# Macaron block on one core: a linear recurrence in groups of two time steps, its tables in PSUM, x loaded by rows and its statistics carried along

## The reference

```python
logits = tokens @ gate_w                       # [4096, 8]
expert_idx = argmax(softmax(logits))
pos = cumsum(one_hot(expert_idx), axis=0) - 1  # place in the expert, kept below 160
h = relu(einsum('ecd,edf->ecf', expert_input, w1))   # 128 -> 512
expert_output = einsum('ecf,efd->ecd', h, w2)        # 512 -> 128
```

```python
Bu = einsum('bsd,nd->bsn', u, B_w)
h_new = ifft(lambdas * fft(h)).real + bu_t      # 512 steps
y = einsum('sbn,dn->bsd', hs, C_w) + D * u
```

## Time and profile before

| | us |
|---|---|
| three runs | 151.61, 151.71, 152.92 (median 151.71) |
| profiled execution: its own time, its span | 150.5, 148.6 |
| busy: PE, PEld, DVE, ACT, POOL | 128.5, 96.6, 88.2, 56.1, 56.0 |
| chain that ended last: PE, DMA, issue, ACT, POOL, DVE | 46%, 14%, 10%, 9%, 7%, 5% of the span |

### The profile page before, as it was taken

How to read it: one execution, slowest core, us unless ns; L and a number is a source line. 1 busy time by engine, 2 the same in 40 slices (tenths; PEclk the granted TensorE clock), 3 DMA queues, 4 the chain that set the end, 5 groups by cost and what they waited for, 6 DMA issues and landing times.

```text
span 148.6 us, 2493 instructions
## 1 busy us (share of the span) xinstructions
PE 128.5 (86%) x749; PEld 96.6 (65%) x749; DVE 88.2 (59%) x379; ACT 56.1 (38%) x156; POOL 56.0 (38%) x96
## 2 busy tenths in 40 slices
PE   5988989699799989379999999999989969999920
PEld 2315334289699965137887788778976249999810
DVE  1198787994467431257679668988894133755310
ACT  2522434235353302055756675752010035553200
POOL 3490002777205778001212211231100677665570
PEclk9999999999999999999999999999995599999995
DMA  4999995236660111690013441344024312211110
GB/s 89 305 351 401 350 290 144 55 108 185 194 203 22 57 53 53 213 321 35 2 45 101 146 133 39 123 148 146 0 76 158 91 46 56 56 38 40 43 45 18
DMA packets 15740, 18.49 MB, mean 124 GB/s; under 512 B 1904, under 2 KB 10608, under 8 KB 15600
## 3 DMA queue, kind: packets, MB, share of 16 engines
q1 hardware_dynamic: 13936, 15.34, 32.7%
q0 software_dynamic: 1280, 2.66, 6.3%
q10 hardware_dynamic: 512, 0.34, 0.9%
HBM read 12.70 MB, written 7.73 MB: 138 GB/s over the span
## 4 chain that ended last, share of the span: by engine, by line
PE 46%; DMA 14%; issue 10%; ACT 9%; POOL 7%; DVE 5%; SPq 4%; POOLq 1%
PE pair L1062 9%; PE pair L1075 9%; ACT u L520 7%; DMA w1s<-w 5%; PE pair L1158 5%; POOL xg L370 5%; PE pair L1149 4%; SPq L292 3%; PE pair L1180 3%; PE pair L1182 3%; PE pair L943 2%; DMA xg<-x,tok 2%; DMA x<-x_scratch 2%; DMA xg<-x_scratch,tok 2%; PE pair L1087 2%
## 5 line engine op out<-in xcount | busy, mean ns | idle before, releaser
L943 PE MATMUL pair<-warm_in,ones_bf 128*128 128x512 bf16 x61 | 18.9, 457 | 3.9 <-DMA x<-x_scratch 2.3
L1062 PE MATMUL pair<-xcT,w1s 128*128 128x160 f32 x128 | 20.5, 303 | 0.6 <-ACT xcT L452 0.6
L1062 PEld LDWEIGHTS pair<-xcT,w1s 128*128 128x128 f32 x128 | 18.0, 190 | 1.7 <-ACT xcT L452 1.7
L460 ACT ACTIVATE hT<-pair 128x320 f32<-128x320 f32 x32 | 13.8, 435 | 13.6 <-PE pair L1062 12.1
L1075 PE MATMUL pair<-hT,w2s 128*128 128x160 f32 x112 | 17.8, 302 | 0.0
L370 POOL DMA_INDIRECT xg<-x,tok x10 | 10.2, 1019 | 16.7 <-issue 16.7
L1075 PEld LDWEIGHTS pair<-hT,w2s 128*128 128x128 f32 x112 | 15.6, 190 | 0.0
L370 POOL DMA_INDIRECT xg<-x_scratch,tok x10 | 10.1, 1007 | 13.7 <-DMA x_scratch<-x 10.9
L943 PEld LDWEIGHTS pair<-warm_in,ones_bf 128*128 128x128 bf16 x61 | 6.8, 117 | 12.2 <-issue 4.1
L402 POOL TENSOR_TENSOR vb<-vq,st 128x128 f32<-128x128 f32 x8 | 3.8, 474 | 27.0 <-ACT vq L495 27.0
L381 POOL DMA_INDIRECT x_scratch<-xnew,tok x10 | 9.9, 985 | 10.3 <-DMA x_scratch<-x 7.6
(11 more groups left out here) (190 smaller groups left out, 242.8 us busy)
## 6 DMA issues: line engine op xcount, KB each, us to landing
x_scratch<-x SPq DMA_DIRECT2D x8, 272.0 KB, 2.1
xt<-x_turned SPq DMA_DIRECT2D x8, 256.0 KB, 6.1
w1s<-w SPq DMA_DIRECT2D x2, 1024.0 KB, 9.0
w2s<-w SPq DMA_DIRECT2D x8, 256.0 KB, 6.7
x_scratch<-x SPq DMA_DIRECT2D x8, 256.0 KB, 3.4
x<-x_scratch SPq DMA_DIRECT2D x8, 256.0 KB, 4.8
out<-x SPq DMA_DIRECT2D x8, 256.0 KB, 2.6
ce<-const_early ACTq DMA_DIRECT2D x1, 330.0 KB, 4.6
```

The lines of the kernel that those rows point to most:

```text
L460: nc.scalar.activation(hT[:, e % 2, half * HC:(half + 1) * HC, :], bank[4 + half][:, 0:HC * CAP] .rearrange("p (c s) -> p c s", c=HC), ACT ...
L943: M(bank[to][:, :], ones_bf[:, :], warm_in[:, :], start=True, stop=True)
L1062: ins = M(bank[4 + half][:, c * CAP:(c + 1) * CAP], w1s[:, i, ch * P:(ch + 1) * P], xcT[:, i * CAP:(i + 1) * CAP], start=True, stop=True)
```

## The change

- **Groups of two** (TR = 2): NG = 256 groups per batch. `group_sums` is two products of 256 columns instead of four of 128; it reads `uT` with a stride. `vq`, `vb`, `va`, `z`, `zs`, `zc`, `state` are 256 wide. `within(b, h)` is, for each half h of the output, one product of 288 columns and one of 144: 864 columns per batch instead of 1392. One level of `powers` more (`p7`).
- **In PSUM**: a copy of `st` (`st_near`) and `zs` lie in bank 7; `va` is written over the group sums in bank 5, so `group_sums(b)` and `gates_within` wait for the scan (`z_r`) instead of for `va`.
- **Order on TensorE**: `group_sums(i)`, `within(i-1, 0)`, `read_out(i-1, 0)`, `turn_u(i+1)`, `within(i-1, 1)`, `read_out(i-1, 1)`. `uT` has three buffers.
- **Order on ScalarE**: `copy_uT(i+1)`, half of `normalise(i+2)`, `turned_part(i+1)`, the other half.
- **Statistics**: x is loaded by rows ahead of w2 into `x1`, whose rows are 134 wide; VectorE takes bn_stats of them between the gathered tiles (steps `x0` to `x7`) into their last six columns, and SyncE stores them to `x1_scratch` instead of the DRAM to DRAM copies. After each `xnew` VectorE takes its bn_stats too, and the scatter waits for that. In the SSM only bn_aggr is left, for batches 2 to 7 ahead of the loop and in i = 0 and 1; `deviation` and `shift` run in four groups instead of eight.
- **w2** is issued behind the gathers: two experts after each of the gathers 0 and 1, and one after each of the gathers 5 to 8. Levels `p0` to `p4` move from ahead of `slots(0)` into its VectorE list.
- **End**: x1 of batch 6 is added by `add_rows(6)` on TensorE and copied out by ScalarE instead of `add_back(6)` on VectorE; `add_rows(7)` goes behind `rank(1, 1)`. `keep_warm(14)` becomes `keep_warm(9)`.

```diff
+    TR = 2
+    NG = SEQ // TR
+    BLOCK = E + PITCH
+    XP = D + 6
...
+        st_near, zs = bank[7][:, 0:NG], bank[7][:, NG:2 * NG]
...
-        dve_steps = [steps("i0 i1 i2 i3 i4 d0 i5 i6 i7 i8 d1 i9 l0 f0 d2 "
-                         "o0 o1 d3 p5 o2 o3 d4 p6 o4 o5 d5 o6 d6 o7 o8 o9"),
+        dve_steps = [steps("x0 x1 i0 x2 i1 x3 x4 i2 x5 i3 x6 d0 i4 x7 i5 p0 i6 p1 i7 p2 i8 p3 d1 i9 l0 f0 d2 "
+                         "o0 o1 p4 d3 p5 o2 o3 d4 p6 o4 o5 d5 o6 d6 o7 o8 o9 p7"),
...
             for b in range(NB):
-                sp.wait_ge(d_gather[min(b + 3, NS - 1)], 16)
-                sp.dma_start(tiles(x1_dram, b), tiles(x_rows, b)).then_inc(d_fill, 16)
+                load_x(b)
+            for j in range(2):
+                sp.wait_ge(d_gather[j], 16)
+                for e in range(j * E // 4, (j + 1) * E // 4):
+                    load_w2(e)
+            for j in range(2, 5):
+                sp.wait_ge(d_gather[j], 16)
+                store_x(j - 2)
+            for j in range(5, 9):
+                sp.wait_ge(d_gather[j], 16)
+                store_x(j - 2)
+                load_w2(j - 1)
+            store_x(LAST)
...
+                def rate_rows(b):
+                    dve.wait_ge(d_x1[b], 16)
+                    for t in range(b * TB, (b + 1) * TB):
+                        ins = V.bn_stats(x1[:, t, D:XP], x1[:, t, 0:D])
+                    ins.then_inc(x_rated, 1)
...
+                        if n == 0:
+                            dve.wait_ge(row_sb, i + 1)
+                            V.bn_stats(xnew[:, i, D:XP], xnew[:, i, 0:D]).then_inc(row_rated, 1)
...
             for i in range(NB):
                 if i + 1 < NB:
                     copy_uT(i + 1)
+                if i == 1:
+                    deviation(3)
                 if i + 2 < NB:
-                    deviation(i + 2)
+                    normalise(i + 2, 0, TB // 2)
                 if i + 1 < NB:
                     turned_part(i + 1)
                 if i + 2 < NB:
-                    normalise(i + 2)
+                    normalise(i + 2, TB // 2, TB)
...
-                V.tensor_tensor(va[:, :], bank[5][:, 0:NG], ct[:, 0:NG], ALU.mult).then_inc(va_r, 1)
+                V.tensor_tensor(bank[5][:, 0:NG], bank[5][:, 0:NG], ct[:, 0:NG], ALU.mult).then_inc(va_r, 1)
...
-                    ins = V.tensor_tensor(zs[dst, :], z[src, 0:NG], st[src, 0:NG], ALU.mult)
+                    ins = V.tensor_tensor(zs[dst, :], z[src, 0:NG], st_near[src, :], ALU.mult)
...
                 if b >= 1:
-                    pe.wait_ge(va_r, b)
-                for c in range(TB):
-                    ins = M(bank[5][:, 0:NG], vt[:, TB - 1 - c, :],
-                            uT[:, b % 2, c * P:(c + 1) * P], start=(c == 0), stop=(c == TB - 1))
+                    pe.wait_ge(z_r, b)
+                by_residue = uT[:, b % 3, :].rearrange("d (h r p) -> d r p h", h=2, r=TR)
+                for r in range(TR):
+                    ins = M(bank[5][:, 0:NG].rearrange("s (p h) -> s p h", h=2), vt[:, TR - 1 - r, :],
+                            by_residue[:, r, :, :], start=(r == 0), stop=(r == TR - 1))
                 ins.then_inc(v_ps, 1)
...
-            keep_warm(14, 7)
+            keep_warm(9, 6)
...
-            for i in range(LAST):
+            for i in range(NB):
                 group_sums(i)
                 if i >= 1:
-                    read_out(i - 1)
-                within_pairs(i)
-                turn_u(i + 1)
+                    within(i - 1, 0)
+                    read_out(i - 1, 0)
+                if i < LAST:
+                    turn_u(i + 1)
+                if i >= 1:
+                    within(i - 1, 1)
+                    read_out(i - 1, 1)
                 if i == NB // 2 + 2:
                     rank(1, 0)
-                within_rest(i)
-            group_sums(LAST)
-            read_out(LAST - 1)
-            within_pairs(LAST)
             gates_within(LAST)
+            within(LAST, 0)
             gates_carried(LAST)
-            within_rest(LAST)
-            read_out(LAST)
+            within(LAST, 1)
+            for h in range(2):
+                read_out(LAST, h)
+            add_rows(LAST - 1)
+            rank(1, 1)
             add_rows(LAST)
-            rank(1, 1)
```

More of the change, by code:

```diff
@@ L528, in _ @@
             turned_part(0)
-            normalise(1)
+            normalise(1, 0, TB // 2)
+            deviation(2)
             for i in range(NB):
@@ L537, in _ @@
                 if i + 2 < NB:
-                    normalise(i + 2)
-            act.wait_ge(x2_ps, 1)
-            nc.scalar.copy(x2[:, LAST * TB:NT, 0:D].rearrange("p (h r) d -> p h r d", h=2), y_of(LAST)[:, :, :, 0:D])\
-                .then_inc(x2_last, 1)
+                    normalise(i + 2, TB // 2, TB)
+            for b in range(LAST - 1, NB):
+                act.wait_ge(x2_ps, b - LAST + 2)
+                nc.scalar.copy(x2[:, b * TB:(b + 1) * TB, 0:D].rearrange("p (h r) d -> p h r d", h=2), y_of(b)[:, :, :, 0:D])\
+                    .then_inc(x2_last, 1)
             slots(1)
@@ L905, in _ @@
             normalise_half(1)
+            stats(2)
+            stats(3)
             for i in range(NB):
                 turn_back(i)
-                if i + 2 < NB:
-                    stats(i + 2)
+                if i < 2:
+                    stats(2 * i + 4)
+                    stats(2 * i + 5)
                 carry(i)
+                if i < 2:
+                    shift(i + 2)
                 turn_forth(i)
@@ L930, in _ @@
             encode_place(1, 1)
-            add_back(LAST - 1)
             index(1)
@@ L1155, in group_sums, with within @@
                 if b >= 1:
-                    pe.wait_ge(va_r, b)
-                for c in range(TB):
-                    ins = M(bank[5][:, 0:NG], vt[:, TB - 1 - c, :],
-                            uT[:, b % 2, c * P:(c + 1) * P], start=(c == 0), stop=(c == TB - 1))
+                    pe.wait_ge(z_r, b)
[3 more added lines that the diff above has]
+                            by_residue[:, r, :, :], start=(r == 0), stop=(r == TR - 1))
                 ins.then_inc(v_ps, 1)
-            def within_pairs(b):
-                if b >= 2:
+            def within(b, h):
+                if b >= 2 and h == 0:
                     pe.wait_ge(x2_r, b - 1)
@@ L1187, in read_out @@
-            def read_out(b):
-                pe.wait_ge(state_r, b + 1)
-                y = y_pair(b)
-                for h in range(2):
-                    ins = M(y[:, h, E:E + 2 * PITCH], state[:, b % 2, :],
-                            gt[:, 2 * h:2 * h + 2, :].rearrange("p r c -> p (r c)"), start=False, stop=True,
-                            skip_group_check=True)
-                ins.then_inc(y_ps, 1)
-            def add_rows(b):
-                pe.wait_ge(d_x1[b], 16)
-                for h in range(2):
-                    ins = M(y_of(b)[:, h, :, 0:D], ident, x1[:, b * TB + 2 * h:b * TB + 2 * h + 2, :], start=False,
+                M(y[:, h, 0:TR * BLOCK], uT[:, b % 3, 2 * h * P:(2 * h + 1) * P], tab[:, :, :].rearrange("p r c -> p (r c)"),
+                  start=True, stop=False, skip_group_check=True)
@@ new lines, in within, with read_out @@
+                ins = M(y[:, h, BLOCK:2 * BLOCK], uT[:, b % 3, (2 * h + 1) * P:(2 * h + 2) * P], tab[:, 0, :],
+                        start=False, stop=False, skip_group_check=True)
+                if h == 1:
+                    ins.then_inc(lag_ps, 1)
+            def read_out(b, h):
+                pe.wait_ge(state_r, b + 1)
+                ins = M(y_of(b)[:, h, :, :], state[:, b % 2, h * P:(h + 1) * P], gt[:, :, :], start=False, stop=True,
+                        skip_group_check=True)
+                if h == 1:
+                    ins.then_inc(y_ps, 1)
@@ L1202, in add_rows @@
+            def add_rows(b):
+                pe.wait_ge(d_x1[b], 32)
+                pe.wait_ge(y_read, LAST)
+                for h in range(2):
+                    ins = M(y_of(b)[:, h, :, 0:D], ident, x1[:, b * TB + 2 * h:b * TB + 2 * h + 2, 0:D], start=False,
                             stop=True, skip_group_check=True)
```

251 lines of the change are left out of this document (119 added, 132 removed).

## The result

The changed kernel takes 159.82 us (median of four runs, 159.03 to 162.22) against 151.66 for the kernel before beside it (four runs): 1.051 times the time, 95% interval 1.043 to 1.059. The profiled execution took 159.03, its span is 157.1 against 148.6, 8.5 more. The forecast was 150.8, the range ended at 153.2: wrong in sign and in size.

A forecast was written before the change was run, and what follows sets the result against it. No single engine was taken as the bound: stages were read separately, the recurrence as a 5.02 us TensorE-ScalarE loop. Terms 0.45 - 1.1 - 0.5 - 2.0 + 2.25 = -0.9 took 151.71 to 150.8 us, range 148.8 to 153.2.

The forecast's parts named there:

- Step 4: First FFN: added VectorE work makes the reload 0.45 late, bounds 0 and 1.9; w2's 1.1 delay mostly made up.
- Rival D: First FFN: w2's first half lands at 36, stage some 2 later, 152.7; chance 0.14 shared with another rival.
- the sign that the prediction named last: First FFN: the first d product waiting past 33 would show the forecast wrong.
- Step 3: Landing of x1 to first turning product: row statistics gone, shorter keep_warm hides behind the rest; -1.1 us.
- Steps 1 and 2: Recurrence: period falls from 5.02 to 4.51, saving 2.0 us; first three batches save 0.5 us.
- The ring: Recurrence: loop setting the period, through TensorE products, then ScalarE's vq copies and two normalise activations; 4.51 us.
- The stride of the reading: group_sums in the recurrence: strided reading taken as no extra cost on 0.90 us, allowing up to a half above.
- Step 5: Tail to last numbering: longer batch latency and VectorE's queue add 2.25 us; number(1, 1) at T(7) + 11.65.
- Step 6: Second gather: waits for index, not the store; change 0, bounds -0.4 and +0.3.
- Rival B: VectorE's queue from batch 4: 256-wide steps cost double, 4.5 per batch, VectorE becomes the bound; 154.6, chance 0.12.

The follow-up runs named there:

- l1: Kernel before with only the changed loading (x ahead of w2, w2 behind the gathers, x stored from SBUF), old recurrence and statistics; 155.69 us, ratio 1.027.
- e5: Changed kernel with nine and six warm products filling TensorE's gaps ahead of tile 2 and the first d; 159.88 us.
- e2: Changed kernel with 22 instead of 16 warm products ahead of the landing of x1; 158.98 us.
- s3: e4 with all four parts of u normalised ahead of the vq copy and shift(2) ahead of carry(0); ratio 1.004.
- recurrence alone: Changed kernel with the loading of the kernel before and row statistics computed after the landing; 154.96 us, ratio 1.026.
- e3: Changed kernel with the first four w2 loads right behind the x loads and 22 instead of 16 warm products; 157.58 us.
- t2: s3 with one warm product ahead of tile 0 (ten meant), 28 ahead of the landing, 7 ahead of the second turning product, and later encoding; ratio 0.992.
- s1: r2 with the first half's encoding behind the loop and more warm products around the landing and ahead of the second turning product; 154.35 us, ratio 1.023.
- l2: Kernel before with only w2 moved behind the gathers, x still copied DRAM to DRAM; 154.72 us, ratio 1.027.
- r2: Recurrence alone with the group sums reading uT in order and writing PSUM with a stride; 156.06 us, ratio 1.028.
- e4: e3 with the group sums reading uT in order and writing PSUM with a stride; one run, 154.15 us.

## Why the prediction was wrong

**Step 4 failed**, on the sentence that TensorE "makes up for most of this 1.1. That is inside the bounds". It priced w2 as late data for one product, and VectorE's added work as the limiter. VectorE wasn't it: without that work l1 lands only 0.8 earlier, and the 0.4 ahead of row 2's scatter is about the 0.45 that the step had for VectorE. The loads delayed what stood beside them: gather 2 took 5.25 to land, TensorE starved, and its clock went to half. 5.55 instead of 0.45. Rival D had the place and the condition (from 33 on; it was 34.81, the sign that the prediction named last), but priced it at 2: it counted neither the late gathers nor the clock, whose share, by the run with the gaps filled (e5), is at least 1.9 of 5.4.

**Step 3**, -1.1, became +0.3: `keep_warm(9)` was scaled from fourteen products at full clock. At half clock it took 3.60 and set T(0) at X + 3.6. With the clock held (e2) T(0) was X + 2.4, near the 2.2 forecast.

**Steps 1 and 2** gave -0.4 instead of -2.5. The ring was right, through `vq` and two activations, and its pieces too (`vq` 0.37, `u` 0.88). The stride of the reading, taken as nothing of a bound up to a half, was 0.2 of 0.9: period 4.67 instead of 4.51, 0.6 over four batches. Most of the rest is T(1) to T(2), 6.0 instead of 4.7 at half clock.

**Step 5** was right in mechanism, +3.3 for 2.25 (its terms add up to 11.5, not 11.65): `va(7)` waits behind `encode`, at T(7) + 6.0 instead of + 5.4, and the scan that `gates_within` waits for ends at T(7) + 7.2 instead of + 6.5. Mis-sized were the VectorE steps: `state`, which reads PSUM and writes in a strided order, 0.61 for 0.42, `zs` 0.87 for 0.8, `number` with `encode` 2.43 for 2.13. GpSimd's `vb` grew from 0.47 to 0.72. By the GPSIMD Engine Reference of the Trainium skill (Elementwise, side-by-side cycle accounting), with its 2.6 cycles an element, the estimate was 0.75; the trace agrees for `vb`, while `zc` grew by less, from 0.56 to 0.73. **Step 6** was right, -0.3 within its bounds.

Rival B had the right engine at the wrong price: a batch costs VectorE 3.4, as the forecast had it, which the ring of 4.67 covers. Once the ring is shorter (s3), with the second routing on top, VectorE has a queue left at T(7). What stays open: why a gap of TensorE is sometimes followed by the lower clock and sometimes not, and so how much of each execution's time it will be; whether a filled gap ahead of tile 0 would keep the clock; and what the bytes of x cost by themselves.

## What to carry to other kernels

When loads are moved, price what they do to the transfers already standing there, gathers above all, not only when they land themselves; a stage that starves TensorE can pay a second time at half clock. Scale a TensorE term from a full-clock row only with a second price, at half clock, beside it, wherever the change lengthens a wait ahead of it. Shortening a ring pays until the engine that does the rest of each turn is full: sum that engine's work over the whole stretch first.

## What the runs showed of the hardware

- The granted clock went to 0.50, the 1.2 GHz level, behind waits of TensorE of 1.92 and 1.15 (changed kernel) and 3.62 (recurrence alone). Behind 2.33 (before) and, in s3, 1.74 it stayed at 1.00. The same wait had both outcomes: ahead of `gates_within` 1.00 behind 1.84 (changed kernel) and 0.50 behind 1.83 (e5); ahead of tile 0 1.00 behind 2.20 (e3) and 0.50 behind 1.94 (t2). Products that compute nothing in the gaps kept it at 1.00 from the landing to the end of the SSM (s1) and through the first products of the FFN (e5).
- With 1 MB of loads issued beside it a gather landed after 5.25 (changed kernel; the median of the ten before was 3.2), and TensorE waited 1.9 to 2.4 for its tile (changed kernel, l1, l2).
- Four passes of 256 columns that read their moving operand alternately from two places 256 elements apart held TensorE for 1.08; read in order and written to PSUM with a stride of two elements, 0.86 (r2, e4).
- On GpSimd a product of 256 columns took 724 to 726 ns, one of 128 474 to 561; on VectorE `va` went from 289 to 433.
